# Attention: the copy of a row's output moves behind the exponential of its step

## The reference

```python
qkv = x @ W_qkv.T                                 # x: (1, 2048, 512), float32
attn = jnp.einsum('bhqd,bhkd->bhqk', q, k) * SCALE
attn = jnp.where(causal[None, None], attn, -jnp.inf)
probs = jax.nn.softmax(attn, axis=-1)
out = jnp.einsum('bhqk,bhkd->bhqd', probs, v)
x = x + _layernorm(out.reshape(b, s, d) @ W_proj.T)
x = x + _layernorm(moe(_layernorm(x)))            # 16 experts, top 6
```

## Time and profile before

| | |
|---|---|
| timed runs | 1801.45, 1806.66, 1807.76 us; median 1806.66 |
| profiled execution | 1801.34 us, of which span 1799.6 us |
| busy in the span | PE 1637.0 (91%), DVE 1194.2 (66%), ACT 1101.9 (61%), POOL 921.9 (51%) |
| exponential (line 647) | 320 times, mean 929 ns |
| copy (line 628) | 64 times, median 594 ns |

### The profile page before, as it was taken

One profiled execution on the slowest core, in us unless ns is written; L12 is line 12 of the kernel. 1 busy time (PEld: TensorE's weight loads), 2 busy tenths in 40 slices (PEclk: granted clock), 3 DMA queues, 4 the chain that ended last, 5 costly groups with the idle time before them and its releaser, 6 DMA issues.

```text
span 1799.6 us, 30739 instructions
## 1 busy us (share of the span) xinstructions
PE 1637.0 (91%) x8959; PEld 1347.8 (75%) x8959; DVE 1194.2 (66%) x2639; ACT 1101.9 (61%) x1653; POOL 921.9 (51%) x748
## 2 busy tenths in 40 slices
PE   6998899999999999999796799999999999999990
PEld 6976566666666666666564799999999999999980
DVE  5523788787887878888478665665665565566544
ACT  2211488787877878787467565665665565556542
POOL 2310388777777877787554333433433443343324
PEclk9999699999999999999997799999999999999995
DMA  7566111111111111110390788888888887788768
GB/s 232 167 193 179 48 48 50 59 52 56 57 47 60 47 48 47 48 48 25 114 350 32 233 247 238 255 247 235 261 246 231 244 228 219 223 244 230 213 166 193
DMA packets 107572, 277.15 MB, mean 154 GB/s; under 512 B 21291, under 2 KB 39083, under 8 KB 100331
## 3 DMA queue, kind: packets, MB, share of 16 engines
q1 hardware_dynamic: 80379, 212.25, 35.5%
q0 software_dynamic: 27056, 63.31, 17.1%
HBM read 194.76 MB, written 63.72 MB: 144 GB/s over the span
## 4 chain that ended last, share of the span: by engine, by line
PE 41%; DVE 3%; POOL 3%; DMA 2%; issue 1%; ACT 1%; POOLq 0%; DVEq 0%; ACTq 0%
PE p_prj L86 24%; PE p_at_ps L86 6%; PE p_logit_ps L86 6%; PE p_ht_ps L1895 3%; PE p_at_ps L1918 2%; DMA m_gate<-acc_rows 1%; DMA acc_rows<-m_y_out,m_row_ids 1%; POOL rows L1287 1%; POOL p_rstd L1273 1%; DVE r_lane_hot L1600 1%; ACT r_edge_hot L1376 1%; DVE p_st L1612 1%; DVE p_st L1606 1%; POOL p_minus L1271 0%; DMA gathered<-h_rows,m_row_ids 0%
## 5 line engine op out<-in xcount | busy, mean ns | idle before, releaser
L611 POOL TENSOR_TENSOR prob_lo<-prob,prob_hi 128x1024 fp32r<-128x1024 f32 x202 | 482.8, 2410 | 174.6 <-DVE prob_hi L705 88.2
L1309 POOL DMA_INDIRECT acc_rows<-m_y_out,m_row_ids x109 | 178.2, 1635 | 417.1 <-ACT m_y_out L1480 388.7
L647 ACT ACTIVATE prob<-a_sp 128x1024 f32<-128x1024 f32 x320 | 292.0, 929 | 111.4 <-PE a_sp L825 71.9
L664 DVE TENSOR_REDUCE part_max<-a_mp 128x1 f32<-128x512 f32 x384 | 262.3, 688 | 55.6 <-PE a_mp L767 51.0
L86 PE MATMUL p_prj<-m_w_hi,m_ht_hi 128*128 128x352 f32 x888 | 297.7, 335 | 1.4 <-DVE m_ht_lo L1709 1.4
L86 PE MATMUL p_prj<-m_w_lo,m_ht_hi 128*128 128x352 f32 x888 | 288.8, 325 | 0.0
L86 PE MATMUL p_prj<-m_w_hi,m_ht_lo 128*128 128x352 f32 x888 | 288.3, 325 | 0.0
L1733 DVE TENSOR_TENSOR m_w_lo<-m_w_raw,m_w_hi 128x704 fp32r<-128x704 f32 (+1 forms) x357 | 270.9, 798 | 22.8 <-ACT m_w_hi L1486 22.4
L1486 ACT ACTIVATE m_w_hi<-m_w_raw 128x704 fp32r<-128x704 f32 (+1 forms) x357 | 229.0, 714 | 16.8 <-PE p_prj L86 16.8
L1719 DVE TENSOR_TENSOR m_at_lo<-p_at_ps,m_at_hi 128x384 fp32r<-128x384 f32 x111 | 61.8, 557 | 252.6 <-ACT m_at_hi L1472 252.6
L634 ACT ACTIVATE prob_hi<-prob 128x1024 fp32r<-128x1024 f32 (+1 forms) x201 | 206.7, 1028 | 6.4
(11 more groups left out here) (230 smaller groups left out, 3356.5 us busy)
## 6 DMA issues: line engine op xcount, KB each, us to landing
m_w_raw<-wexp SPq DMA_DIRECT2D x51, 1408.0 KB
m_w_raw<-wexp SPq DMA_DIRECT2D x51, 768.0 KB
qk_parts<-rows SPq DMA_DIRECT2D x64, 256.0 KB, 3.0
multi<-qk_parts SPq DMA_DIRECT2D x84, 128.0 KB, 2.7
acc_rows<-p_zeros SPq DMA_DIRECT2D x2, 4352.0 KB, 17.2
v_head<-v_all SPq DMA_DIRECT2D x16, 520.0 KB, 3.0
k_stack<-qk_parts SPq DMA_DIRECT2D x48, 128.0 KB, 2.5
q_stack<-qk_parts SPq DMA_DIRECT2D x48, 128.0 KB, 2.7
```

Of the source, the lines that this page charges most:

```text
L611: nc.gpsimd.tensor_tensor(prob_lo[:, t % RING, :, c0:NB], prob[:, t % RING, :, c0:NB], f32(prob_hi[:, t % RING, :, c0:NB]), ALU.subtract). ...
L647: nc.scalar.activation(prob[:, t % RING, :, c0:NB], sp_[:, t % 2, :, c0:NB], ACT.Exp, scale=SCALE).then_inc(prob_ready, 1)
L664: nc.vector.reduce_max(part_max[:, qb, kb:kb + 1], mp[:, n % 2, 0:width], AX_X).then_inc(piece_done, 1)
L1309: nc.gpsimd.indirect_dma_start(acc_dram[sum_of(t)], bass.IndirectOffsetOnAxis(ap=row_id(t), axis=0), y_out[:, t % 4, :], None, compute_op= ...
```

## The change

In ACT's head function the two conditional calls of `copy_out` move from ahead of the waits and the exponential of their step to behind them, ahead of the step's high part. The waits of each call move with it.

```diff
             def head(h, p, visit, first, last):
                 for t, (j, kp, c0) in enumerate(S_TILES):
+                    act.wait_ge(scores_ready, h * NS + (t + 1))
+                    if not (first and t < RING):
+                        act.wait_ge(pv_done, h * NS + (t + 1 - RING))
+                    nc.scalar.activation(prob[:, t % RING, :, c0:NB], sp_[:, t % 2, :, c0:NB], ACT.Exp,
+                                         scale=SCALE).then_inc(prob_ready, 1)
                     if t == J_LAST[-1] + LAG - NS and not first:
                         copy_out(h * NTB - 1, NTB - 1, h * NS)
                     for jj in range(NTB - 1):
                         if t == J_LAST[jj] + LAG:
                             copy_out(h * NTB + jj, jj, h * NS + (J_LAST[jj] + 1))
-                    act.wait_ge(scores_ready, h * NS + (t + 1))
-                    if not (first and t < RING):
-                        act.wait_ge(pv_done, h * NS + (t + 1 - RING))
-                    nc.scalar.activation(prob[:, t % RING, :, c0:NB], sp_[:, t % 2, :, c0:NB], ACT.Exp,
-                                         scale=SCALE).then_inc(prob_ready, 1)
                     high_part(h, t)
```

## The result

| | before | after |
|---|---|---|
| median of 20 runs each | 1803.3 us | 1808.09 us |
| ratio, 95% interval | | 1.0028 (1.0019 to 1.0037) |
| profiled execution's span | 1799.6 us | 1803.8 us |
| attention, first exponential to last copy | 195.94 to 860.03 us, 664.1 | 200.05 to 865.84 us, 665.8 |

The change costs 0.28%, about 5 us. That lies in the range and inside "within 0.5%", on the side that was forecast, at twice the forecast size (2.4 us).

A forecast was written before the change was run, and what follows sets the result against it. Attention heads were taken as bound by a POOL and DVE chain until step 11, then by PE. Step 15's +2.9 less the last head's 0.5 gave +2.4 us on 1804.3: 1806.7 us, range 1796.1 to 1811.4.

The forecast's parts named there:

- step 15: Copy behind exp(15) starts 0.18 us later (0.25 in unrolled heads), PE too, nothing absorbs it: 2.9 us lost.
- What bounds a head: Up to PE's wait at 597.56, POOL's low parts and DVE's lo(8) and maximum; from there PE leads until step 18.
- Step 5: Copy behind exp(5) lets PE go 0.54 us earlier, fourteen times, 7.6 us; booked at nothing, absorbed by the wait at 597.56.
- Both waits at step 6 "go": PE's waits of 0.60 us for step 5's copy and 0.16 us for exp(4) were both to vanish.
- The last head: Tail waits 0.54 us for POOL's lo(18); exp(16) comes earlier, so up to 0.5 us gained, bounds 0 and 0.54.
- Twelve heads in the loop look alike: Twelve loop heads were taken to look like the one followed near 575 us; three or four near the ends differ.
- The port rival: Step 18: DVE's lo(17) starts before POOL's lo(18), PE's 0.34 us wait goes; -1.7 to -3.0 us; chance 0.30.
- Relieved wait counts: Rival: POOL's chain does not hold 597.56, so step 5's 7.6 us stay; -5.2 us, 1799.1 us; chance 0.13.
- the copy later than the overlap: Rival: copy starts only after the exponential's signal, step 15 loses 0.31 us in 15 heads; +4.7 us, 1809.0; chance 0.12.

The follow-up runs named there:

- uncovered pair: Kernel before with tile 9's high part on ACT and POOL's lo(7), lo(18) held for DVE: copies first 1805.5 us; copies of steps 3, 5, 9 moved 1794.4 us.
- doubled dose: Kernel before with only step 15's copy moved, behind the exponential of step 16 too: 1819.2 us, ratio 1.0082.
- filling the wait: Kernel before with copies of steps 3, 5, 9 moved and PE computing tile 11's scores twice, except in the last head: 1805.4 us, ratio 1.0005.
- before_filled: Kernel before, with PE computing the scores of tile 11 twice in all heads but the last: 1804.3 us, ratio 0.9997.
- after_filled: Changed kernel, with PE computing the scores of tile 11 twice in all heads but the last: 1807.1 us, ratio 1.0018.

## Why the prediction came out as it did

**The result** was right in sign and range, and its size was 2.4 us where 4.8 were measured. The sign is in part luck: the only loss in the sum, step 15, measured 1.8 us by itself, and in the timed executions the clock takes 75.7 us where it takes 72.4 to 74.0 in the kernel before, so 2 to 3 of the 4.8 us are a cost that the sum did not have. The points in turn:

- *What bounds a head* (POOL's chain until step 11, then PE). Right: PE's wait at step 11 grew by what step 6 saved. The uncovered pair shows the other half, that the saving counts once the cover is off.
- *Step 15, 0.18 us a head, 2.9 us in all.* Right in mechanism: 0.12 to 0.27 us a head in the trace. Alone it measured 1.8 us (0 to 3.6), and the doubled dose fits.
- *Step 5 "booked at nothing".* **This is the step that failed**, and its price was over zero: moved without step 15, the three copies cost 7.4 us. I had found where the saved time would go, a wait of 1.4 us instead of 0.84, and priced a longer wait behind a cover at zero, because the sum of PE's time is the same. The clock made the difference: filling the wait brings the 7.4 us down to 0.9, and the clock's part from 78.9 to 72.3 us.
- *Both waits at step 6 "go".* Wrong in wording, right in number: 0.27 to 0.67 us of waiting stay, since PE arrives earlier too; its next multiplication is 0.56 us earlier.
- *The last head, up to 0.5 us of gain.* Its passage takes 32.57 instead of 33.33 us, but the clock of the kernel before falls in it, at 845 us, and that of the changed one does not. In before_filled and after_filled, whose last heads are as in these two and have no fall, it takes 32.83 and 32.55: a gain of 0.28 us.
- *Twelve heads in the loop look alike.* They don't: before, those of the first half take 41.0 us and those ahead of the jump back 42.1 to 42.8. The sum does not change by it, but PE's longest standstills in the loop of the kernel before lie behind the jump, in step 3.
- *The port rival, 0.30.* It occurred in part: 5 of 14 heads. The margin was read rightly (0.02 to 0.07 us in the loop, but for the head with the fall). The wait saved was put at 0.34 to 0.45 us in each head, less the 0.18 of the delay; measured it is 0.64 us, but in the heads of the loop's first half alone.
- *Relieved wait counts* (0.13) did not happen, *the copy later than the overlap* (0.12) neither: the copy starts 0.90 us after its exponential. That rival's 4.7 us is near the measured loss by accident.

**What stays open.** The single moves (1.8 and 7.6 us) add up to more than the change (4.8). In the clock's part they do add up, within its error: 2.7 us less, 5.2 more, and 2 to 3 more for the whole. DVE is first in five heads of the profile after, and three of these are 0.6 us shorter by it; the rest lies within the intervals, 1.8 us each way for the first move alone and 2.5 for the second.

## What to carry to other kernels

A wait that is hidden behind another engine's chain is not free to lengthen: when several short waits of TensorE are relieved and their time gathers in one place, look at the granted clock behind that place, and compare the clock of before and after stretch by stretch, not only busy times. One profile has few falls, and what one costs depends on where it stands, so set the mean granted clock of all timed executions beside it. Take off the cover first and then relieve the wait; in the reverse order the same edit measured as a loss of 5 us and would have been thrown away, and behind the other it was part of a kernel that is 0.5% faster. Where two engines hold each other up and start within 0.2 us of each other, fix the order with a wait rather than leave it to the race; here one added wait gained 6 us.

## What the hardware showed that I had not expected

- A fall of TensorE's granted clock from 2.4 to 1.2 GHz after single standstills of 0.9 to 1.6 us in a stage where PE is busy over 90% of the time, up to five in 580 us. Each lasts about 3.4 us and takes 1.7 us of clock; it cost 1.5 us of time in step 11, and well under 1 us where a wait behind it could absorb it.
- Of POOL's and DVE's two-input instructions the one with the earlier recorded start does not always go first: at a lead of POOL of 0.02 us DVE did, at 0.03 POOL.
- DVE's cast with a single input is held up by POOL as the subtraction with two is: 2.10 against 0.68 us.
